# Idle multiplications on TensorE: 42 places with 921 of them instead of 36 places with 649, in a transformer kernel of 16 sequences

## The reference, cut to what matters

```
block 0: m = silu(cond) @ w_ada + b_ada              # nine shifts, scales and gates
  h = ln(x)*(1+sc)+sh;  x += g * (window_attention(h) @ w_so + b_so)       # "w": windows of 128, shifted by 64
  h = ln(x)*(1+sc)+sh;  x += g * (top16_cross_attention(h, ctx) @ w_co)    # "t": 16 best scores of each row
  h = ln(x)*(1+sc)+sh;  x += g * (silu(h@w_a) * (h@w_b)) @ w_m2            # "m": hidden width 1024
block 1 ("l"): q from adaptive_ln(x), k and v from adaptive_ln(ctx), 16 heads of 16
  out = x + (softmax(q k^T / 4) v @ Wp + bp)
```

## Time and profile before

| what | before |
|---|---|
| median of 3 runs | 1324.44 us (1323.28 to 1324.77) |
| the profiled execution, its own time | 1324.96 us |
| its span, first to last instruction | 1323.2 us |
| mean granted TensorE clock over the span | 0.975 |
| TensorE (PE) busy | 1218.7 us, 92% |
| VectorE (DVE) busy | 1146.4 us, 87% |
| ScalarE (ACT) busy | 997.5 us, 75% |
| GpSimd (POOL) busy | 882.3 us, 67% |

### The profile page before, as it was taken

How to read it: one execution, slowest core, us unless ns; L and a number is a source line. 1 busy time by engine, 2 the same in 40 slices (tenths; PEclk the granted TensorE clock), 3 DMA queues, 4 the chain that set the end, 5 groups by cost and what they waited for, 6 DMA issues and landing times. The chain is left out here.

```text
span 1323.2 us, 39161 instructions
## 1 busy us (share of the span) xinstructions
PE 1218.7 (92%) x13841; PEld 863.0 (65%) x13841; DVE 1146.4 (87%) x3819; ACT 997.5 (75%) x2001; POOL 882.3 (67%) x1161
## 2 busy tenths in 40 slices
PE   5688799999999999999999999999999999989987
PEld 5565576667676666667676767666666766656664
DVE  3359999999999999999999999999999999896222
ACT  3534587869797988979797979788797978767844
POOL 2324397858686786958595968869595957666720
PEclk9688999999999999999999999999999999999998
DMA  4450111202121121202131211212111211110010
GB/s 155 125 155 14 41 54 32 72 22 68 40 57 42 48 60 38 70 23 69 27 77 31 58 34 44 56 42 73 33 48 37 57 36 34 34 41 10 25 26 25
DMA packets 111391, 67.27 MB, mean 51 GB/s; under 512 B 13836, under 2 KB 107870, under 8 KB 111198
## 3 DMA queue, kind: packets, MB, share of 16 engines
q1 hardware_dynamic: 111198, 64.76, 18.4%
HBM read 22.33 MB, written 4.19 MB: 20 GB/s over the span
## 5 line engine op out<-in xcount | busy, mean ns | idle before, releaser
L1249 ACT ACTIVATE prob<-turned_score 128x1024 f32<-128x1024 f32 x320 | 325.9, 1018 | 107.5 <-PE turned_score L948 102.4
L1479 POOL TENSOR_TENSOR pair<-full,pair 128x512 f16<-128x512 f32 x192 | 222.2, 1165 | 129.1 <-ACT pair L1223 124.0
L1387 DVE TENSOR_REDUCE rowmax_l<-score 128x4 f32<-128x1024 f32 x128 | 156.0, 1219 | 62.6 <-PE score L948 49.4
L1400 DVE MATCH_REPLACE8 rest<-top,score 128x256 f32<-128x256 f32 x512 | 207.7, 413 | 0.0
L1414 DVE MATCH_REPLACE8 far<-best,rest 128x256 bf16<-128x256 f32 x512 | 205.2, 408 | 0.0
L1485 POOL TENSOR_SCALAR far<-far 128x512 bf16<-128x512 bf16 x256 | 158.0, 617 | 70.0 <-DVE far L1414 49.9
L1397 DVE MAX8 top<-score 128x8 f32<-128x256 f32 x512 | 192.2, 416 | 6.6 <-PE score L948 6.6
L948 PE MATMUL work<-pair_n,w_m_hi 128*128 128x256 f16 x1024 | 174.2, 275 | 1.6 <-issue 1.5
L948 PE MATMUL work<-pair_n,w_m_lo 128*128 128x256 f16 x512 | 140.3, 274 | 0.0
L1223 ACT ACTIVATE pair<-full 128x512 f16<-128x512 f32 x192 | 121.0, 630 | 17.4
L1464 POOL TENSOR_SCALAR rstd_n<-mean_var_n 128x2 f32<-128x2 f32 x64 | 13.1, 205 | 175.5 <-DVE mean_var_n L1379 173.3
(11 more groups left out here) (199 smaller groups left out, 3168.9 us busy)
## 6 DMA issues: line engine op xcount, KB each, us to landing
q_stack_w<-pair SPq DMA_DIRECT2D x96, 64.0 KB, 2.3
k_stack_w<-pair SPq DMA_DIRECT2D x96, 64.0 KB, 2.3
k_stack_t<-pair SPq DMA_DIRECT2D x96, 64.0 KB, 2.3
q_stack_t<-pair SPq DMA_DIRECT2D x96, 64.0 KB, 2.3
k_stack_l<-pair SPq DMA_DIRECT2D x96, 64.0 KB, 2.3
q_stack_l<-pair SPq DMA_DIRECT2D x96, 64.0 KB, 2.3
ctx_t<-in_ctx_turned SPq DMA_DIRECT2D x16, 256.0 KB, 2.9
ctx_l<-in_ctx SPq DMA_DIRECT2D x16, 256.0 KB, 2.9
```

What stands on the lines that cost most here:

```text
L1249: act.activation(prob[:, at:at + 2, :], both_b[:, :, :], ACT.Exp).then_inc(exp_done, 1)
L1387: dve.tensor_reduce(rowmax[s][n % 2][:, :].rearrange("p (z m) -> p z m", z=2)[:, :, at:at + wide], both_a[:, :, :].rearrange("p z (h k) -> ...
L1400: m = dve.match_replace(rest[p % 2][:, t, :], eight[:, t, :], bank[:, t * L:(t + 1) * L], -FAR)
L1479: pool.tensor_tensor(pr[:, 1, :, :], whole[:, :, :], pr[:, 0, :, :], ALU.subtract).then_inc(split_lo, 1)
```

## The change

Only the text `IDLE_WORK` changes. Each of the 36 entries gets about a third more multiplications, and six entries are new: `wp:0:17=7`, `a_w:3:0=13`, `bk_l:12:0=9`, `pr_t:15:0=8`, `o_l:13:2=7`, `ot_l:13:0=7`. The sum goes from 649 to 921. 19 of the old entries stand in the first 175 us of the profiled execution, 17 in its last 105 us, and the sequences between have none in either kernel; of the new ones `a_w:3:0` lies at 198 us and `bk_l:12:0` at 1198 us.

```
-IDLE_WORK = ("x4_n1:0:0=7 a_w:0:0=11 a_w:0:2=21 bk_w:0:0=18 pr_w:0:0=7 x4_n2:0:0=26 a_w:1:2=19 a_t:0:0=21 "
-             "a_w:1:3=18 a_t:0:1=27 a_t:0:2=31 a_t:0:4=36 a_t:0:5=19 xt_w:1:0=17 a_w:2:2=18 a_t:1:0=22 "
-             "bk_t:0:0=19 x4_n3:0:0=23 a_t:1:4=8 bk_t:15:0=14 x4_n4:14:0=14 xt_t:15:0=17 a_l:14:3=15 "
-             "bk_l:13:0=7 pr_l:13:0=13 m2:15:2=12 xt_m:15:0=17 pj_lq:15:0=14 o_l:14:2=11 a_l:15:0=36 "
-             "bk_l:14:0=10 a_l:15:3=9 a_l:15:7=14 o_l:15:3=17 bk_l:15:0=18 pr_l:15:0=43")
+IDLE_WORK = ("x4_n1:0:0=10 a_w:0:0=15 a_w:0:2=28 bk_w:0:0=24 pr_w:0:0=9 x4_n2:0:0=35 wp:0:17=7 a_w:1:2=26 "
+             "a_t:0:0=28 a_w:1:3=25 a_t:0:1=36 a_t:0:2=41 a_t:0:4=48 a_t:0:5=26 xt_w:1:0=23 a_w:2:2=24 "
+             "a_t:1:0=30 bk_t:0:0=25 x4_n3:0:0=30 a_t:1:4=11 a_w:3:0=13 bk_l:12:0=9 bk_t:15:0=19 x4_n4:14:0=18 "
+             "pr_t:15:0=8 xt_t:15:0=23 o_l:13:2=7 a_l:14:3=21 ot_l:13:0=7 bk_l:13:0=9 pr_l:13:0=18 m2:15:2=16 "
+             "xt_m:15:0=23 pj_lq:15:0=18 o_l:14:2=15 a_l:15:0=48 bk_l:14:0=13 a_l:15:3=12 a_l:15:7=19 "
+             "o_l:15:3=23 bk_l:15:0=24 pr_l:15:0=57")
```

## The result

The kernel after takes 1328.08 us (median of 12 runs, 1323.64 to 1330.05), the kernel before 1324.41 us (median of 12, 1319.7 to 1327.23). The measured ratio is 1.0033, with a 95% interval of 1.0021 to 1.0045: the change costs 4.4 us, between 2.8 and 6.0. That is slower by more than the 0.2% that can be told from no change.

A forecast was written before the change was run, and what follows sets the result against it. PE and DVE pace the middle, PE and a chain through ACT, POOL and SyncE the end. Tail 2.3 plus start-up 0.5 less clock 0.5 gave +2.3 us: 1327.3 profiled, 1326.7 us as median, range 1322.3 to 1329.4.

The forecast's parts named there:

- rival A: Tail and start-up: all overruns delay real work and no clock comes back; +4.6 us, 1329.0 us; chance 0.25.
- The rates: All idle groups: one multiplication to the next takes 56 ns at full clock, 107 ns at half clock.
- The tail, +2.3: From 1200 us on: old groups longer than their pauses sum to 2.63 us, taken as 2.3; bounds 1.6 and 3.1.
- pj_lq:15: Tail group of 14 at 1273.44 us: 4 added multiplications delay the real work at half clock, 107 ns each.
- The slack of 0.3: Tail: pieces behind seven groups show up to 0.1 us of slack each, some 0.3 us taken off.
- The start-up, +0.5 - 0.5 = 0: Start-up: longer groups cost +0.5 us (bounds 0.2 and 2.3), clock won back gives -0.5.
- the 1.6 us of a_w:1:2, a_w:1:3, a_t:0:5 and x4_n3:0: Start-up: 28 more multiplications, 1.6 us whole, put at nothing because pauses and DVE's backlog cover them.
- the 0.24 us that I read as free ahead of a_w:2:2: Start-up group at 143.70 us: 6 added at half clock take 0.64 us, 0.24 of it free, so +0.4.
- the clock won back at 47 us: Start-up: 7 added multiplications at 44.2 us keep the clock up through 50.5 us, -0.5 us.
- The DMA cover at 74 to 85 us: Start-up: filling the stretch ahead of the fall at 74.4 gains nothing, since a DMA chain sets the pace; at most 3.1 us.
- B: Tail and start-up: the clock falls vanish, -2.6 to -3.6 us, 1320.8 us; chance 0.15.
- C: Whole kernel: new work lies in real pauses, or gains and overruns cancel; within 1 us, 1324.4; chance 0.22.

The follow-up runs named there:

- tight_longer: Kernel before with only the 16 groups that already filled their pauses raised to the change's counts (97 more multiplications); ratio 1.0042, +5.6 us.
- tail_only: Kernel before with the change's longer groups in the tail only, start-up as before; ratio 1.0015, +2.0 us (0 to 4.1).
- start_only: Kernel before with the change's longer groups in the start-up only, tail as before; ratio 1.0028, +3.7 us (1.6 to 5.8).
- the late ones: Fourteen groups from 85 to 199 us; kernel before with the change's counts only there (108 more multiplications): ratio 1.0014, +1.9 us (0.4 to 3.4).
- tight_shorter: Kernel before with the 16 groups that already filled their pauses made shorter by the change's step (90 fewer multiplications); ratio 1.0004, +0.5 us.
- two_thirds_more: Kernel before with its 36 groups lengthened by twice the change's step, six new ones as in the change, 1142 multiplications; ratio 1.0111, +14.7 us.
- three_groups_less: Kernel before without the groups ahead of x4_n3:0, pr_l:13 and m2:15:2 (48 multiplications fewer); ratio 0.9992, -1.1 us (-2.6 to 0.5).
- the tight and the roomy halves: Kernel before with the change's counts only for 16 groups filling their pauses (1.0042, +5.6 us), or only for 26 with room (1.0023, +3.0 us).

## Why the prediction was right, and where it was short

- **The sign and the mechanism.** I forecast +2.3 us, within 0.2%, in a range of 1322.3 to 1329.4, and gave "same" the largest chance. The measured +4.4 (2.8 to 6.0) lies in the range, but is nearly twice the forecast and near rival A (+4.6): the overruns pass, and little clock comes back. The mechanism that the forecast and A share, that a group longer than its pause delays the real work, is what tight_longer shows most directly, 5.6 us for 5.4 us of multiplications.
- **The rates** of 56 and 107 ns held. The trace after, with 48 in 2.79 us on the chain, leaves no place for the 81 ns of the Trainium skill, "TensorE: Matmul & The Clock Gate", section "Back-to-back issue gap"; 48 of those would last 3.9 us.
- **The tail, +2.3.** tail_only gave +2.0 (0 to 4.1), the profiled tails +1.9. The total fits, within a wide interval; its parts fit only at full clock. The five groups at full clock grew by 1.28 us on the chain after, where I had 1.29. Of the two at half clock, pj_lq:15 ran at full clock after, 18 in 1.09 us where 14 had taken 1.49: 0.40 less in place of 0.43 more. That execution has one fall of 3.4 us in the tail where before had one of 3.4 and one of 6.8, and its tail is only 0.2 us longer than before. The slack of 0.3 that I took off was hardly there: a score piece starts 0.15 us behind the last idle start even when it waits for nothing. By the same token a_l:15:0 had 0.29 us free and not 0.44. And ot_l:13, which I had put at nothing beside a row maximum, is on the chain after, 7 in 0.50 us.
- **The start-up, +0.5 - 0.5 = 0.** This term failed. start_only gave +3.7 (1.6 to 5.8). Four of its steps don't hold. First, I put the 1.6 us of a_w:1:2, a_w:1:3, a_t:0:5 and x4_n3:0 at nothing, since DVE's backlog would cover them. They are among the tight groups, which cost their whole length, and among the late ones, which cost 1.9; no run has them alone. Second, the 0.24 us that I read as free ahead of a_w:2:2 is what a score piece shows at half clock without any wait: 0.24 or 0.25 us behind 12, 18, 24 and 30 idle multiplications alike, in tight_shorter, before, after and two_thirds_more. Third, I read the room of each pause from one execution, and two pauses with 0.7 to 0.8 us there had 0.15 in three_groups_less. Fourth, I booked the clock won back at 47 us as a gain of 0.5; the fall came 1.5 us later (48.6 after) and lasted 10.2 us as before, so the clock at 1.00 from 47 to 50 us didn't come, and over the whole start-up it is 0.88 against 0.87.
- **The DMA cover at 74 to 85 us.** In the main this held. The modulation of wp:0:17 ran at full clock, the projection behind it began at 76.22 instead of 78.38, and the `k_stack_w` and `q_stack_t` issues did not follow by that much, as the timeline of SyncE after shows beside the earlier trace rows:

```profile
75.77 3.81 SPq L918 DMA_DIRECT2D k_stack_w<-pair  x6
83.76 0.38 SPq L893 DMA_DIRECT2D hid<-in_L_xcond_Wq  x1
84.25 3.75 SPq L918 DMA_DIRECT2D q_stack_t<-pair  x6
```

They are 0.40 and 0.56 us earlier, where the projection is 2.16 earlier (1.62 of it because the modulation itself began earlier); 0.56 is just over the 0.5 that I had set. The first top-16 scores came 0.65 us later than before and not earlier, behind a group of 28 with no wait. What I missed is the next fall: where PE finished early it stood idle for longer, and the fall behind that was longer and caught the next modulation.
- **The middle** has the busy times of before, as forecast; in the profiled executions it is 2.5 us shorter after, for which see the last section. The new groups there delay nothing: behind the piece ahead of them a_w:3:0 started after 1.06 us before and 1.11 after, bk_l:12:0 after 0.48 in both.
- **A sign of being wrong that came.** I had written that fewer stretches at 0.50 in the tail would show me wrong. The execution after has one where that of before has two, and by the runs' mean clocks the change takes 3 to 6 us out of the time at half clock. So some clock did come back in places where I had none, and the overruns must have cost more than 4.4 us, by up to half of those 3 to 6 (an estimate from the clocks). That the sum stayed in the range is in part luck: the start-up came out at 3.7 where I had 0, and the two ends measured apart sum to 5.7, which would have lain beyond it.
- **Rivals.** B, the falls vanish and the kernel gets faster, is out by the interval, though the tail's falls did go from two to one in the profiled execution. C is out by the interval. What stays open: why the tight and the roomy halves sum to 8.6 us, which single group in the first 85 us costs most, and what the four groups called covered cost by themselves.

## What to carry to other kernels

Idle work ahead of a known pause pays for its clock only as long as it ends before the pause does; here half to the whole of the old length was equally good, and a third more cost 4.4 us. Leave room, since a pause read from one execution may be its longest, and look at the granted clock by stage: here, once it had stopped rising with more idle work, five sixths of what was added came out as delay. A stage that runs faster than its DMAs need can make a longer pause behind it; here the clock's next fall then lasted longer, on work that was not covered.

## What the runs showed that was not expected

Two executions of one kernel differ by up to 0.6% (before: 1319.7 to 1327.2 us in 12 runs), and the clock's falls differ in place and number: the profiled execution of before had falls at 272, 1091 and 1180 us in an otherwise full middle, that after only one, at 274, and its middle is 2.5 us shorter. Over the profiled executions the middle's length, from a_w:3:0 to bk_l:12:0, goes with these falls and not with the idle work: 994.5 and 994.7 us with none, 994.3 to 996.9 in six with one of 3.4 us (999.0 in a seventh, that with 1142), 998.8 to 999.4 in the three with three. The runs say the same: of the 35 runs of before on one chip, the five with a mean granted clock of 0.982 took 1319.5 to 1320.6 us, the four with 0.973 took 1324.4 to 1327.6. The profiled executions' spans therefore say little about a change of 4 us.
